# Expert weights issued by SyncE instead of ScalarE in the routing, the fourth group held until the first rows are in

## The chip, the cores and the metric

The kernel runs on one core of a Trainium2 chip. The time is the device time of one execution in microseconds (us). Engines: PE is TensorE, DVE is VectorE, ACT is ScalarE, POOL is GpSimd and SP is SyncE. A name with a q (ACTq, SPq) is an engine's instruction queue, where it issues transfers or waits.

## The reference

Eight layers in a row work on x, 1250 rows of 512 numbers: four graph convolutions and, behind each, a feed-forward layer. Each adds its result to x. Three of the feed-forward layers send rows to experts (a mixture of experts):

```
L0_ffn: attention; 64 experts (512 -> 256 -> 512), top 2 of a softmax, 78 places each; y weighted by the gates
L2_ffn: 8 experts (512 -> 512 -> 512), the best one only, no limit of places
L3_ffn: attention; 8 experts (512 -> 256 -> 512), top 2, 250 places each, each row keeps its last expert
```

In each of them the router's logits are xn @ wr, a softmax and the largest entries give every row its experts, and the expert computes func(rows @ w1 + b1) @ w2 + b2.

## The kernel before

The program is a sequence of blocks. In a block every engine has an instruction stream of its own, and the streams wait for each other by semaphores; at a block's end all engines meet. A routed layer has three blocks that matter here.

`norm_rows` norms the rows and transposes them. In L0_ffn and L3_ffn its ACT stream also issues the load that brings x back from a copy in DRAM (L404).

`route` (L1098) computes the assignment. SP writes the normed rows to DRAM (L1173, 2.5 MB in two transfers) and waits for them (L1174). PE makes the logits (L1181), DVE takes the maxima off (L1231), ACT makes the exponentials (L1216), DVE continues from L1233 with sums, the largest entries, one-hot masks (L1253) and the residual (L1916), PE counts places (L1191, L1192), DVE and PE make the list of rows of each unit (L1295, L1202), and ACT copies the gates (L1219). ACT's stream begins with `early(act)` (L1214), which is `issue_first` of the weights.

`experts` (L1434) works in units. A unit is two sets of R rows (R is 78 in L0_ffn, 125 in L2_ffn and L3_ffn). POOL gathers each set from the DRAM copy with one indirect transfer into `xb` (L1532); in L0_ffn and L3_ffn four units are gathered ahead, in L2_ffn one. PE transposes the rows (L1612), DVE moves them to `xbT` (L1684, in L2_ffn L1680), PE multiplies by w1 (L1623), ACT applies the function (L1657), PE multiplies by w2 (L1632), DVE copies out (L1693) and POOL scatters the result (L1542). In L0_ffn and L3_ffn PE transposes the second unit ahead of the products of the first (`run_ahead`, L1485); in L2_ffn, where the number of units is only known at run time, there is one unit at a time.

Weights lie in a ring of four groups (`ExpertBuffers`, L1394). A group is two experts in L0_ffn (four transfers of 512 KB), one expert in L2_ffn (two of 1 MB) and in L3_ffn (two of 512 KB). A group serves one unit in L0_ffn and L3_ffn, and one or more in L2_ffn. `issue_first` (L1423) issues the table b1 and three groups: 13 transfers in L0_ffn, 7 in L2_ffn and in L3_ffn. The fourth group, and later each group that has been used up, is issued by ACT in its loop in `experts` (`weights`, L1646), the fourth as the first thing of the block, since its semaphore `w_used` is raised there at once (L1599, L1600).

Of the kernel before, what the change touches and what calls it, by code (L numbers as in the profile page):

```python
# [352 lines left out]
def in_two(dst, src):  # L353

    return [(dst[0:120], src[0:120]), (dst[120:P], src[120:P])]
# [318 lines left out]
def attention(nc, k, x1, w_qk, b_qk, Vall, ctxT, room, spare, spare_free, late_loads, sums_dram):  # L674
# [11 lines left out]
    with ExitStack() as ctx:  # L686
# [62 lines left out]
        with nc.Block() as block:  # L749
# [245 lines left out]
            def _(v):  # L995
# [63 lines left out]
                def invert(h):  # L1059

                    v.wait_ge(sums_in, h * 32 + 32)
                    v.reciprocal(sums[:, 1, :], sums[:, 0, :]).then_inc(inv_ready, 1)
# [32 lines left out]
                take_projections(1, 1)  # L1095
                schedule(v, tiles, between)
                invert(*last[0])
def route(nc, k, yT, wr, br, E_, topk, cap, keep_last, r, rows_in, early=None, meanwhile=None):  # L1098

# [3 lines left out]
    with ExitStack() as ctx:  # L1105
# [47 lines left out]
        with nc.Block() as block:  # L1153
            @block.gpsimd
            def _(pool):
                pool.iota(ioE[:, :], [[1, E_]], base=0, channel_multiplier=0,
                          allow_small_or_imprecise_dtypes=True).then_inc(iotas, 1)

                for c in range(topk):
                    pool.iota(token1[:, c, :], [[P, T]], base=c * N + 1, channel_multiplier=1,  # L1160
                              allow_small_or_imprecise_dtypes=True).then_inc(iotas, 1)
                pool.iota(ioR[:, :], [[1, R]], base=0, channel_multiplier=0,
                          allow_small_or_imprecise_dtypes=True).then_inc(iotas, 1)
                pool.iota(no_row[:, :], [[R, NB]], base=r.unused + 1, channel_multiplier=1,
                          allow_small_or_imprecise_dtypes=True).then_inc(iotas, 1)
                if cap is None:
                    pool.iota(ioU[:, :], [[R, NB]], base=0, channel_multiplier=0,
                              allow_small_or_imprecise_dtypes=True).then_inc(iotas, 1)

            @block.sync  # L1170
            def _(sp):
                for to, what in in_two(rowtiles(r.rows_dram), rows_in):
                    sp.dma_start(to, what).then_inc(r.rows_out, 16)  # L1173
                sp.wait_ge(r.rows_out, 32)  # L1174

            @block.tensor
# [33 lines left out]

            @block.scalar
            def _(act):
                if early is not None:
                    early(act)  # L1214
                act.wait_ge(shifted, 1)
                act.activation(W[:, :, :], L[:, :, :], ACT.Exp).then_inc(exps, 1)  # L1216
                act.wait_ge(gT_done, 1)
                for n, (c0, cn) in enumerate(CH):
                    act.activation(r.gateT[:, c0:c0 + cn], ps[0:E_, 5 + n, 0:cn], ACT.Copy).then_inc(gT_out, 1)  # L1219
# [174 lines left out]
class ExpertBuffers:  # L1394
# [16 lines left out]
        self.b1s = sb("b1s", [128, E_, self.FC])  # L1411
        self.w_in = [ctx.enter_context(k.semaphore(nc, k.name(f"w_in{g}"))) for g in range(self.RING)]

    def issue(self, act, i, g):

        for x_ in range(self.EPG):
            e, slot = (i * self.RING + g) * self.EPG + x_, g * self.EPG + x_
            act.dma_start(self.w1s[:, slot, :, :], self.w1[bass.ds(e, 1)].rearrange("o p c f -> p (o c) f"))\
                .then_inc(self.w_in[g], 16)
            act.dma_start(self.w2s[:, slot, :, :], self.w2[bass.ds(e, 1)].rearrange("o (c p) n -> p (o c) n", p=128))\  # L1420
                .then_inc(self.w_in[g], 16)

    def issue_first(self, act):  # L1423

        act.dma_start(self.b1s[:, :, :], self.b1).then_inc(self.w_in[0], 16)
        for g in range(self.RING - 1):
            self.issue(act, 0, g)

    def loaded(self, eng, i, g):

# [3 lines left out]
def experts(nc, k, r, wts, func, affine, y_dram, dynamic, x, b2, Y, out=None):  # L1434
# [13 lines left out]
    with ExitStack() as ctx:  # L1448
# [15 lines left out]
        rows_loaded = [[k.gpsimd_dma_semaphore(nc, "rows") for _ in range(2)] for _ in range(DEEP)]  # L1464
# [9 lines left out]
        def group(eng, i, g, body):  # L1474

            e = i * RING + g
            if dynamic:
                n = eng.snap(eng.value_load(r.tab[0:1, 0, bass.ds(e, 1)], min_val=1, max_val=N // (2 * P)))
                first = eng.snap(eng.value_load(r.tab[0:1, 1, bass.ds(e, 1)], min_val=0, max_val=r.max_blocks))
                with eng.Fori(0, n) as q:  # L1480
                    body(i, first + q, g)
            else:
                body(i, e, g)
# [31 lines left out]
        def second(s):  # L1515
            return s if EPG == 2 else 0

        with nc.Block() as block:
# [62 lines left out]
            def loads(eng, c):  # L1581
                eng.wait_ge(all_stored, 1)
                src = rowtiles(y_dram[c * N:c * N + N, :])
                for h in range(PIECES):
                    for to, what in in_two(Y[c][:, TP * h:TP * h + TP, :], src[:, TP * h:TP * h + TP, :]):
                        eng.dma_start(to, what).then_inc(got[h], 16)  # L1586
# [57 lines left out]
            @block.scalar  # L1644
            def _(act):
                def weights(i, g):  # L1646
                    act.wait_ge(w_used[g], i + 1)
                    wts.issue(act, i, g)

                def hidden_at(i, g):  # L1650

                    def hidden(i, u, g):
                        for s in range(2):
                            act.wait_ge(h_done[s], u + 1)
                            e = (i * RING + g) * EPG + second(s)
                            for m in range(FC):
                                act.activation(hT[:, s, m, :], ps[:, 4 * s + 1, R * m:R * m + R], func,  # L1657
                                               bias=wts.b1s[:, bass.ds(e, 1), m]).then_inc(h_out[s], 1)
                    group(act, i, g, hidden)

                with act.Fori(0, ROUNDS - 1) as i:
                    for g in range(RING):
                        weights(i + (1 if g else 0), (g + RING - 1) % RING)
                        hidden_at(i, g)
                weights(ROUNDS - 1, RING - 1)
                for g in range(RING):
                    hidden_at(ROUNDS - 1, g)
                if K_ == 2:
                    loads(act, 1)
# [76 lines left out]
def rowtiles(ap):  # L1746

    return ap.rearrange("(t p) n -> p t n", p=P)
# [119 lines left out]
def transformer(nc, k, a, x128, pre, E_, F, cap, func, keep_last, rows_dram, y_dram, x_spill, sums_dram, out=None):  # L1868

    with ExitStack() as ctx:  # L1870
# [39 lines left out]
        with ExitStack() as c4:  # L1910
            wts = ExpertBuffers(nc, k, c4, E_, F, R, 1 if R == cap else 2, a[pre + "w1_p"], a[pre + "b1_p"],
                                a[pre + "w2"], Room(Gf))

            def add_residual(v):
                v.wait_ge(x_back, 32)
                v.tensor_tensor(x[:, :, :], x[:, :, :], res[:, :, :], ALU.add)  # L1916
            route(nc, k, xnT, wr, br[:, :] if bias else None, E_, 2, cap, keep_last, r, yn, wts.issue_first, add_residual)
            experts(nc, k, r, wts, func, (g2, b2), y_dram, False, x, b2r[:, :], (res, yn), out)
# [273 lines left out]
def l2_ffn(nc, k, a, x, rows_dram, y_dram):  # L2192

    E_, F = 8, 512
    with ExitStack() as ctx:
        def sb(c_, name, shape):
            return c_.enter_context(nc.sbuf_tensor(k.name(name), shape, fp32))
        xn, xT = sb(ctx, "xn", [P, T, D]), sb(ctx, "xT", [128, C, N])
        b2r, wr, br = sb(ctx, "b2r", [E_, D]), sb(ctx, "wr", [128, C, E_]), sb(ctx, "br", [1, E_])
        norm_rows(nc, k, x, xn, xT, have_stats=True, beside=[(wr[:, :, :], kchunks(a["L2_ffn_Wr"])), (br[:, :], row(a["L2_ffn_br"])),  # L2200
                                            (b2r[:, :], a["L2_ffn_b2"])])
        r = Routing(nc, k, ctx, E_, 1, None, P, rows_dram)
        with ExitStack() as c4:
            wts = ExpertBuffers(nc, k, c4, E_, F, P, 2, a["L2_ffn_w1_p"], a["L2_ffn_b1_p"], a["L2_ffn_W2"])
            route(nc, k, xT, wr, br[:, :], E_, 1, None, False, r, xn, wts.issue_first)
            experts(nc, k, r, wts, ACT.Relu, None, y_dram, True, x, b2r[:, :], (xn,))
# [338 lines left out]
```

## Time and profile before

| | us |
|---|---|
| median of 3 runs | 3326.5 (3324.61 to 3326.77) |
| profiled execution | 3323.3 |
| its span in the trace | 3321.5 |
| PE busy (share of the span) | 2699.4 (81%) |
| DVE busy | 1683.2 (51%) |
| ACT busy | 943.7 (28%) |
| POOL busy | 277.6 (8%) |
| mean granted TensorE clock | 0.891 |

Busy times are sums over all stages, and each stage has its own limit. Instructions that issue transfers are not counted as busy. The routing of L0_ffn starts at about 1267.6 in the span, that of L2_ffn at 2206.7 and that of L3_ffn at 3137.8. In a row, a bracket gives the idle time of the engine ahead of the group and what ended it.

### The profile page before, as it was taken

What the parts mean: (1) busy time and instruction counts of PE and PEld (TensorE: products, weight loads), DVE (VectorE), ACT (ScalarE), POOL (GpSimd) and SP (SyncE); (2) the same over time, 40 slices, a digit from 0 to 9 for tenths busy, and PEclk for the clock granted to TensorE, in tenths of its full rate; (3) what the DMA queues carried; (4) which work ended last, traced back from release to release, by engine and by line L of the source; (5) the groups of instructions that cost most, each with busy time, mean ns of one, the idle gap of its engine ahead of it and who ended that gap; (6) DMA issues with size and microseconds to landing.
All of it is one profiled execution on the core that took longest, in us unless ns stands there. A gap on an engine that the chain in (4) does not pass through costs nothing. (4 is left out here: it accounts for less than half of the span.)

```text
span 3321.5 us, 41255 instructions
## 1 busy us (share of the span) xinstructions
PE 2699.4 (81%) x12659; PEld 1899.7 (57%) x12660; DVE 1683.2 (51%) x3356; ACT 943.7 (28%) x2087; POOL 277.6 (8%) x273
## 2 busy tenths in 40 slices
PE   5888869985899984999688599967877579999775
PEld 3555555554778853666365266665644457877452
DVE  6777752133788834444533722241132458886344
ACT  1222230102577731111111022210111237777100
POOL 0000000000000001444000000002210000000031
PEclk9999979997899986999798799967978789999767
DMA  3000041202000005798413130033333110000334
GB/s 103 1 0 0 0 141 39 60 4 65 13 23 18 16 9 181 262 303 296 113 46 128 27 74 13 0 108 101 99 83 60 44 34 19 18 19 13 99 117 117
DMA packets 113512, 237.85 MB, mean 72 GB/s; under 512 B 32500, under 2 KB 33860, under 8 KB 112130
## 3 DMA queue, kind: packets, MB, share of 16 engines
q10 hardware_dynamic: 47350, 126.49, 12.8%
q1 hardware_dynamic: 41740, 82.14, 8.5%
q0 software_dynamic: 24320, 27.90, 2.9%
q8 instruction: 60, 0.98, 0.1%
q14 instruction: 42, 0.34, 0.0%
HBM read 189.78 MB, written 52.58 MB: 73 GB/s over the span
## 5 line engine op out<-in xcount | busy, mean ns | idle before, releaser
L1050 DVE TENSOR_REDUCE mx<-ps 125x1 f32<-125x500 f32 (+1 forms) x480 | 274.0, 588 | 57.0 <-PE ps L820 40.2
L243 PE MATMUL ps<-onehot_src,onehot_dst 125*128 x1200 | 257.7, 353 | 42.1 <-DVE onehot_dst L219 16.9
L945 ACT ACTIVATE probs_hi<-ps 125x500 fp32r<-125x500 f32 (+1 forms) x480 | 255.4, 532 | 123.8 <-DVE probs_lo L1002 79.1
L218 DVE TENSOR_SCALAR onehot_src<-iota,src_f 125x1250 f16 x400 | 217.4, 544 | 108.6 <-PE ps L243 95.7
L947 ACT ACTIVATE x<-ps 125x500 f32<-125x500 f32 (+1 forms) x480 | 258.7, 539 | 0.0
L1002 DVE TENSOR_TENSOR probs_lo<-x,probs_hi 125x1250 fp32r<-125x1250 f32 x160 | 240.2, 1501 | 35.8 <-ACT x L947 32.2
L1693 DVE COPY yb<-ps 78x512 f32<-78x512 f32 (+1 forms) x100 | 68.9, 689 | 325.7 <-PE ps L1632 325.7
L243 PEld LDWEIGHTS ps<-onehot_src,onehot_dst 125*128 x1200 | 120.9, 102 | 172.5 <-issue 117.7
L1632 PE MATMUL ps<-w2s,hT 128*78 128x512 f32 (+1 forms) x480 | 215.9, 596 | 1.9 <-ACT hT L1657 1.9
L820 PE MATMUL ps<-K_hi_lo,Q_hi_twice 128*125 128x500 f32 (+1 forms) x480 | 181.3, 384 | 23.0 <-DVE mx L1050 17.8
L828 PE MATMUL ps<-Q_hi_twice,K_hi_lo 128*125 128x500 f32 (+1 forms) x480 | 178.9, 373 | 17.9 <-ACT Q_lo_max L935 5.1
L1657 ACT ACTIVATE hT<-ps,b1s 128x78 f32<-128x78 f32 (+1 forms) x240 | 67.0, 342 | 408.3 <-PE ps L1623 408.2
L978 POOL TENSOR_TENSOR room<-room 64x600 f32 (+1 forms) x16 | 32.6, 2040 | 1780.3 <-DMA inv<-sums 1780.3
L829 PE MATMUL ps<-Q_lo_max,K_hi_one 65*125 65x500 f32 (+1 forms) x480 | 176.1, 368 | 0.0
L836 PE MATMUL ps<-probs_hi,V_hi 125*128 125x500 f32 (+1 forms) x480 | 174.0, 362 | 0.0
L837 PE MATMUL ps<-probs_hi,V_lo 125*128 125x500 f32 (+1 forms) x480 | 165.5, 360 | 0.0
L1773 PE MATMUL ps<-w,xT 128*125 128x512 f32 x320 | 145.8, 618 | 16.8 <-ACT xT L2121 8.9
L424 PE MATMUL ps<-ident,xn 125*128 125x125 f32 x280 | 45.9, 344 | 139.5 <-DVE xn L394 139.5
L1623 PE MATMUL ps<-xbT,room 128*128 128x78 f32 (+1 forms) x1280 | 154.6, 281 | 0.6 <-issue 0.6
L1623 PEld LDWEIGHTS ps<-xbT,room 128*128 128x128 f32 x1280 | 151.2, 197 | 2.3 <-issue 2.3
L219 DVE SCALAR_TENSOR_TENSOR onehot_dst<-iota,dst_f,w_parts x400 | 137.1, 343 | 0.0
L1632 PEld LDWEIGHTS ps<-w2s,hT 128*78 128x78 f32 (+1 forms) x480 | 76.5, 168 | 103.0 <-issue 101.1
(368 smaller groups left out, 4783.4 us busy)
## 6 DMA issues: line engine op xcount, KB each, us to landing
room<-in_L_ffn_w_p ACTq DMA_DIRECT2D x72, 512.0 KB, 6.0
w2s<-in_L_ffn_w ACTq DMA_DIRECT2D x72, 512.0 KB, 8.4
G<-c_spill ACTq DMA_DIRECT2D x2, 5859.4 KB
tv<-in_L_ffn_tv_W_p SPq DMA_DIRECT2D x2, 4096.0 KB
w1s<-in_L_ffn_w_p ACTq DMA_DIRECT2D x8, 1024.0 KB, 4.9
w2s<-in_L_ffn_W ACTq DMA_DIRECT2D x8, 1024.0 KB, 9.5
w_spill<-W SPq DMA_DIRECT2D x5, 1171.9 KB
c_spill<-CT ACTq DMA_DIRECT2D x1, 5859.4 KB
```

Source lines behind the costliest of these rows:

```text
L218: v.tensor_scalar(ohs[:, slot, :].rearrange("p o n -> p (o n)"), io16[:, 0:N], sF[:, bass.ds(tile, 1)], None, ALU.is_equal)
L243: mm_ = pe.matmul(ps[:, 3 * half + c, 0:cn], ohd[:, slot, :].rearrange("p o n -> p (o n)"), ohs[:, slot, c0:c0 + cn].rearrange("p o n -> p ...
L820: pe.matmul(ps[0:P, SQ + cc % 2, 0:cn], Q1[:, j, P * t:P * t + P], K1[:, j, c0:c0 + cn], start=True, stop=True).then_inc(s_done, 1)
L828: pe.matmul(o, K1[:, j, P * t:P * t + P], Q1[:, j, c0:c0 + cn], start=True, stop=False)
L829: pe.matmul(o, K2[:, j, P * t:P * t + P], Q2[:, j, c0:c0 + cn], start=False, stop=True)\
L836: pe.matmul(ps[:, ACC + n, 0:cn], VH[:, t, :], PH[:, t % 2, c0:c0 + cn], start=(t == 0), stop=False)
L945: act.activation(PH[:, t % 2, c0:c0 + cn], ps[0:P, ST + n, 0:cn], ACT.Exp, scale=SCALE).then_inc(p_hi, 1)
L947: act.activation(PT[:, t % 2, c0:c0 + cn], ps[0:P, ST + n, 0:cn], ACT.Exp, scale=SCALE).then_inc(p_out, 1)
L1002: v.tensor_tensor(PL[:, t % 2, :], PT[:, t % 2, :], PH[:, t % 2, :].bitcast(fp32), ALU.subtract)\
L1050: v.tensor_reduce(mx[:, t, n:n + 1], ps[0:P, SQ + cc % 2, 0:cn], AX.X, ALU.max)\
L1623: mm = pe.matmul(ps[:, 4 * s + 1, R * m:R * m + R], wts.w1s[:, w, c, 128 * m:128 * m + 128], xbT[:, s, parity, c, :], start=(c == 0), stop ...
L1632: mm = pe.matmul(ps[0:R, 4 * s + 2, :], hT[:, s, m, :], wts.w2s[:, w, m, :], start=(m == 0), stop=(m == FC - 1))
```

## The change

`early` is called in SP's stream, behind the issues of the row store and ahead of the wait for it, and no longer at the head of ACT's stream. In `experts` ACT waits, ahead of its loop, for both sets of rows of the first unit; its first issue behind that wait is the fourth group of weights. All three routed layers are changed.

```diff
-def route(nc, k, yT, wr, br, E_, topk, cap, keep_last, r, rows_in, early=None, meanwhile=None):
+def route(nc, k, yT, wr, br, E_, topk, cap, keep_last, r, rows_in, early, meanwhile=None):
...
                 for to, what in in_two(rowtiles(r.rows_dram), rows_in):
                     sp.dma_start(to, what).then_inc(r.rows_out, 16)
+                early(sp)
                 sp.wait_ge(r.rows_out, 32)
...
             @block.scalar
             def _(act):
-                if early is not None:
-                    early(act)
                 act.wait_ge(shifted, 1)
...
-    def issue_first(self, act):
-
-        act.dma_start(self.b1s[:, :, :], self.b1).then_inc(self.w_in[0], 16)
+    def issue_first(self, sp):
+
+        sp.dma_start(self.b1s[:, :, :], self.b1).then_inc(self.w_in[0], 16)
         for g in range(self.RING - 1):
-            self.issue(act, 0, g)
+            self.issue(sp, 0, g)
...
+                for s in range(2):
+                    act.wait_ge(rows_loaded[0][s], 16)
                 with act.Fori(0, ROUNDS - 1) as i:
                     for g in range(RING):
                         weights(i + (1 if g else 0), (g + RING - 1) % RING)
```

`issue` has the name of its first argument changed from `act` to `eng` and is otherwise as it was.

## Rows read from the trace of the kernel before

**Rows 1.** Order of time, routing of L0_ffn: start us, duration us, engine, line, tiles, count.

```profile
1267.61 2.21 SPq L1173 DMA_DIRECT2D rows<-yn  x2
...
1278.46 0.82 DVE L1231 TENSOR_TENSOR logits<-pos,m 125x640 f32<-125x640 f32 x1
...
1284.81 1.28 ACT L1216 ACT_TABLE_LOAD   x1 [17.46 <-issue]
1286.10 0.74 ACT L1216 ACTIVATE work<-logits 125x640 f32<-125x640 f32 x1
1286.87 0.82 DVE L1233 TENSOR_REDUCE m<-work 125x10 f32<-125x640 f32 x1 [7.58 <-ACT work L1216]
```

**Rows 2.** Order of time, start of the experts of L0_ffn, and PE's fourth unit.

```profile
1316.35 0.35 ACTq L1418 DMA_DIRECT2D room<-in_L_ffn_w_p  x1
1316.57 1.16 POOL L1532 DMA_INDIRECT xb<-rows,take  x1 [48.24 <-issue]
...
1320.55 0.96 POOL L1532 DMA_INDIRECT xb<-rows,take  x1 [0.30 <-issue]
...
1329.31 7.04 PE L1623 MATMUL ps<-xbT,room 128*128 128x78 f32 x32
...
1358.18 3.74 PE L1623 MATMUL ps<-xbT,room 128*128 128x78 f32 x32
```

**Rows 3.** Order of time, routing of L2_ffn and start of its experts.

```profile
2219.28 1.28 ACT L1216 ACT_TABLE_LOAD   x1 [12.88 <-issue]
...
2228.33 0.24 DVE L1231 TENSOR_TENSOR logits<-pos,m 125x80 f32<-125x80 f32 x1
2228.60 0.27 ACT L1216 ACTIVATE work<-logits 125x80 f32<-125x80 f32 x1 [8.04 <-DVE logits L1231]
...
2257.33 1.24 POOL L1532 DMA_INDIRECT xb<-rows,unit  x1 [0.97 <-POOL unit L1525]
2258.88 1.22 POOL L1532 DMA_INDIRECT xb<-rows,unit  x1 [0.30 <-issue]
...
2267.39 1.93 PE L1612 MATMUL ps<-ident,xb 125*128 125x125 f32 x8 [13.02 <-DMA xb<-rows,unit]
```

**Rows 4.** Order of time, routing of L3_ffn and start of its experts.

```profile
3161.72 0.27 ACT L1216 ACTIVATE work<-logits 125x80 f32<-125x80 f32 x1 [11.79 <-DVE logits L1231]
...
3189.86 1.27 POOL L1532 DMA_INDIRECT xb<-rows,take  x1 [51.43 <-issue]
...
3194.48 1.21 POOL L1532 DMA_INDIRECT xb<-rows,take  x1 [0.30 <-issue]
...
3202.29 5.47 PE L1623 MATMUL ps<-xbT,room 128*128 128x125 f32 x32
```

**Rows 5.** Transfer issues, us to landing: first gather of L0_ffn, L2_ffn and L3_ffn.

```profile
xb<-rows,take POOLq DMA_INDIRECT x1, 7.2
...
xb<-rows,unit POOLq DMA_INDIRECT x1, 10.0
...
xb<-rows,take POOLq DMA_INDIRECT x1, 7.7
```

**Rows 6.** Same, median: L0_ffn from 1327.5, 1350 to 1580; L2_ffn from 2275; L3_ffn 3196 to 3205.

```profile
xb<-rows,take POOLq DMA_INDIRECT x2, 4.7
...
xb<-rows,take POOLq DMA_INDIRECT x52, 6.8
...
xb<-rows,unit POOLq DMA_INDIRECT x16, 5.3
...
xb<-rows,take POOLq DMA_INDIRECT x6, 5.7
```

**Rows 7.** Busy us by stretch; then granted clock, DMA share, GB/s.

```profile
1297.00:1316.00 19.00, 10.41 (x89) 9.87 (x88) 15.44 (x28) 1.32 (x3) 0.00 (x0) 0.62 0.00 0
1329.00:1336.00 7.00, 7.00 (x36) 7.00 (x35) 2.17 (x8) 1.82 (x3) 0.07 (x1) 0.50 0.26 60
2208.00:2214.00 6.00, 6.00 (x32) 5.87 (x32) 0.00 (x0) 0.00 (x0) 0.00 (x0) 0.60 0.98 216
```

More of the change, by code:

```diff
@@ L1412, in __init__, with issue @@
         self.w_in = [ctx.enter_context(k.semaphore(nc, k.name(f"w_in{g}"))) for g in range(self.RING)]
-    def issue(self, act, i, g):
+    def issue(self, eng, i, g):
         for x_ in range(self.EPG):
             e, slot = (i * self.RING + g) * self.EPG + x_, g * self.EPG + x_
-            act.dma_start(self.w1s[:, slot, :, :], self.w1[bass.ds(e, 1)].rearrange("o p c f -> p (o c) f"))\
+            eng.dma_start(self.w1s[:, slot, :, :], self.w1[bass.ds(e, 1)].rearrange("o p c f -> p (o c) f"))\
                 .then_inc(self.w_in[g], 16)
-            act.dma_start(self.w2s[:, slot, :, :], self.w2[bass.ds(e, 1)].rearrange("o (c p) n -> p (o c) n", p=128))\
+            eng.dma_start(self.w2s[:, slot, :, :], self.w2[bass.ds(e, 1)].rearrange("o (c p) n -> p (o c) n", p=128))\
                 .then_inc(self.w_in[g], 16)
-    def issue_first(self, act):
-        act.dma_start(self.b1s[:, :, :], self.b1).then_inc(self.w_in[0], 16)
+    def issue_first(self, sp):
+        sp.dma_start(self.b1s[:, :, :], self.b1).then_inc(self.w_in[0], 16)
         for g in range(self.RING - 1):
-            self.issue(act, 0, g)
+            self.issue(sp, 0, g)
     def loaded(self, eng, i, g):
```

## The prediction

> **What bounds the kernel now.** One core runs some thirty stages one after another. TensorE is busy for 81% of the span, but what this change can move lies where TensorE stands idle, so I read the page first for the size of the whole and then the order of time of three short stretches: the three routings (in L0_ffn, L2_ffn and L3_ffn) and the start of the experts behind each. In these, every wait that ends last was looked up.
>
> In the routing of L0_ffn the reader sees a straight chain on VectorE and one gap in it. The maxima are taken off the logits (L1231) from 1278.46 for 0.82 us, so the exponential may start at 1279.3. ScalarE is not there: it is still issuing the b1 table and three groups of weights, 13 transfers, 17.46 us of "issue"; then it loads its table (1.28 us), and only at 1286.10 runs Exp. VectorE stood idle 7.58 us [rows 1]. In the other two routings the same issuing is hidden: the products of the router take so long that ScalarE waits for VectorE, 8.04 us in L2_ffn [rows 3] and 11.79 us in L3_ffn [rows 4]. The table load there follows the issuing at once and ahead of the wait (2219.28 against 2228.60), so it hides as well [rows 3].
>
> At the start of the experts all three stand still for one thing: the gathered rows. In L0_ffn GpSimd issues at 1316.57 and the first products start only at 1329.31 [rows 2]. In L2_ffn the PE waits 13.02 us for its first rows [rows 3]. In each case ScalarE issued the fourth group of weights just ahead of the gathers (1316.35 against 1316.57), so 2 MB in L0_ffn and L2_ffn, 1 MB in L3_ffn, run beside the first rows. The first gathers take 7.2, 10.0 and 7.7 us to land [rows 5]; ones with little or nothing beside them take 4.7, 5.3 and 5.7 us [rows 6].
>
> **Part 1: the issuing moves to SP.** On ScalarE 13 + 7 + 7 issues go away. In L0_ffn Exp can start 0.03 us behind L1231, as it does in L2_ffn (2228.33 + 0.24, then 2228.60) [rows 3]: 1279.28 + 0.03 + 0.74 + 0.03 puts L1233 at 1280.08 against 1286.87 [rows 1]. That is 6.8 us. The table load moves to about 1267.7, under the router's products. VectorE's chain from there to the end of the routing has no other wait that this time could run into: the residual is added meanwhile (its x was fetched in the stage ahead of the routing), and the rest alternates between VectorE and PE. I count 6.8 us in full, and 0 for the 7 issues in each of L2_ffn and L3_ffn, whose cover is 8.04 and 11.79 us.
>
> SP pays for it. It issues the two pieces of the row store, then the 13 (7, 7) weights, and only then waits for the store. Were its issues as slow as ScalarE's, it would be through at 1267.6 + 2.21 + 17.2 = 1287, while the routing ends at about 1308.5 in the new time: 21 us of cover. Nobody else waits for SP before that end. The weights now stand behind the store on one queue. In the six microseconds from 2208, when the store of L2_ffn was most of the traffic, 216 GB/s moved; even if store and weights (2.5 + 6.3 MB) went at that rate to the end, the last group would be in 41 us behind 1267.6, at 1309, and the first products of the experts want the first group only at about 1320. Today DMA is at rest from 1297 on [rows 7]. Cost: 0 (between 0 and, if the cover went, microsecond for microsecond).
>
> **Part 2: the fourth group waits for the first unit's rows.** Times from GpSimd's first gather (t0).
>
> L0_ffn: gathers start at 0 and, the fourth, 3.98 us; so the second at about 1.4 [rows 2]. At 4.7 us each [rows 6] the first unit is there at 6.1, ScalarE issues until about 8, and the second unit's last rows, issued before that but landing beside its first packets, come at 3.98 + 5.2 = 9.2. The value 5.2 is mine: from 4.7 (quiet) to 6.8, the median of the 52 gathers beside a steady stream of weights [rows 6]. With 1.1 us of transposes the products start at t0 + 10.3 where they started at 12.74 [rows 2]: 2.4 us, between 0.8 and 2.9.
>
> L2_ffn: both gathers of the unit (0 and 1.55 us) precede the products and no other does. 1.55 + 5.3 + 1.0 for the last four transposes = 7.9, against 10.06 for the landing and 1.9 for the eight transposes, 11.9 in all [rows 3, 6]: 4.0. The first gather of a stage may start slower than later ones, so 3.8, between 2 and 4.7.
>
> L3_ffn: 1 MB only was in the way. The fourth gather starts 4.62 us behind the first, + 5.7 + 1.1 of transposes = 11.4, against 12.43 to the products [rows 4, 6]: 1.0, between 0 and 2.
>
> What stands behind the new wait on ScalarE: the fourth group's issues (1.85 us in L0_ffn, four of about 0.4 with their gaps), then the activations of the first unit. Those need the PE's first products, at t0 + 10.3 or later; ScalarE is free again at 6.1 + 1.85 = 8, so nothing is late. The fourth group itself is first read by the fourth unit, whose products started 41.6 us behind t0 (1358.18) [rows 2]; issued at 6 to 8 and landing in at most ten or so, it has over 20 us in hand. Cost: 0.
>
> The Trainium skill's page "DMA: Bandwidth & Descriptors" (Anatomy of one DMA) gives 2.0 us plus the bytes at 436 GB/s for a GpSimd transfer; an estimate by it is 2.4 to 2.6 us for such a gather. By that the three starts would give some 7 us more in all, 3305 us. No row here supports it: the quiet ones took 4.7 us and more [rows 6].
>
> **The sum.** 6.8 + 2.4 + 3.8 + 1.0 = 14.0 us. The profiled execution took 3323.3 us (span 3321.5 and 1.8 around it), so 3309.3; the median of the runs shown is 3326.5, 3.2 above it, and carrying that along the forecast is 3312.5 us, 0.42% faster.
>
> **The rivals.**
> A. *The gathers don't get quicker.* Their 7 to 10 us could be the first use of the queue in a stage rather than the weights: in each case only the first gathers are slow, and they are first as well as crowded. For it: in L3_ffn 1 MB and in L0_ffn 2 MB give nearly the same (7.7, 7.2) [rows 5]. Against: the steady gathers beside weights also take longer (6.8) than quiet ones (4.7) [rows 6]. Only the 6.8 us remain: 3319.7. Chance 0.14.
> B. *The 7.58 us gap is handed on.* VectorE arrives 6.8 us sooner, but something in the routing holds its end: SP still at its issues, or the store's landing. Then only the starts gain, 7.2 us: 3319.3. Against: 21 us of cover. Chance 0.05.
> C. *The PE's clock helps too.* The first unit of L0_ffn runs at a granted clock of 0.50, the lower level of 1.2 GHz [rows 7], and its 32 products take 7.04 us against 3.74 in the fourth unit [rows 2]. If less idle time ahead kept the higher level, the unit would gain up to the 3.3 us there, and the first unit of L3_ffn, whose 32 take 5.47 us [rows 4], somewhat less than 2: 3307. Against: even quiet, seven microseconds stay idle ahead of it. A small shift either way (1 to 2 us) is likelier and is in my range. Chance 0.08.
> D. *Slower: weights late behind the store.* On one queue the first group could reach the chip after the experts ask for it. It decides once it lands later than t0 + 10 (1320), and makes the whole slower by 0.2% only from 1341 on (14.0 + 6.7 us later); the queue would then have averaged some 120 GB/s over 73 us. Against: 216 GB/s [rows 7]. It would give about 3334. The same skill page (Queues, rings and completion order) says that each DMA engine takes a queue's descriptors in order and alternates between queues, so it speaks for the weights starting later; no run shows yet how much. Chance 0.03.
>
> **How the numbers follow.** The forecast has 0.70: 14.0 us with bounds 6.8 + 0.8 + 2 + 0 = 9.6 and 6.8 + 2.9 + 4.7 + 2 = 16.4, two more either way for the clock, 3308 to 3319. With the upper end drawn out to A and B and the lower to C: 3307 to 3320. About 0.2% (6.7 us, 3319.8) is what a measurement of this kernel can tell from no change. A sits on that edge and gives half of its chance to "same"; part of B too. Faster 0.88, same 0.09, slower 0.03.
>
> **What would show it.** Right: in the routing of L0_ffn Exp starts within 0.1 us of L1231's end and the routing is some 7 us shorter; SP carries the 13 issues and is through well before it; ScalarE issues the fourth group 6 to 7 us behind t0; the first gather lands in 5 us or so; the PE's wait in L2_ffn shrinks from 13 to about 9 us. Wrong: gathers still at 7 to 10 us with no weights under way (A); SP the last to end the routing (B); a PE wait for w_in in front of L1623 (D).

## The result, and the profile after

Six executions of each, alternating on one chip: 3305.2 us after (3298.2 to 3308.0) against 3325.6 before (3319.9 to 3329.5). The ratio is 0.9942, 95% interval 0.9932 to 0.9951: 19.3 us faster, 16.3 to 22.6. The forecast was 14.0 us and 3312.5; the time lies 1.8 us below the range. The profiled execution took 3304.6 us, with a span of 3302.6 and a mean granted clock of 0.895.

The routing of L0_ffn in the order of time, changed kernel (the edit moves most line numbers up by one: L1231 is L1230 now, L1623 is L1622):

```profile
1267.18 1.75 SPq L1173 DMA_DIRECT2D rows<-yn  x2
1267.19 1.28 ACT L1215 ACT_TABLE_LOAD   x1 [0.27 <-PEq L377]
...
1268.98 2.60 SPq L1424 DMA_DIRECT2D b1s<-in_L_ffn_b_p  x1
...
1278.04 0.83 DVE L1230 TENSOR_TENSOR logits<-pos,m 125x640 f32<-125x640 f32 x1
...
1278.90 0.74 ACT L1215 ACTIVATE work<-logits 125x640 f32<-125x640 f32 x1 [10.42 <-DVE logits L1230]
1279.67 0.82 DVE L1232 TENSOR_REDUCE m<-work 125x10 f32<-125x640 f32 x1 [0.80 <-ACT work L1215]
...
1288.04 0.59 SPq L1419 DMA_DIRECT2D w2s<-in_L_ffn_w  x1
```

The 7.58 us in front of the sum of the exponentials [rows 1] are 0.80 now, which is Exp itself. The engine that waits has changed: ScalarE stands 10.42 us for VectorE. SP's last issue is at 1288.04, twenty microseconds ahead of the end of the block.

The start of the experts of L0_ffn, same view:

```profile
1309.38 1.16 POOL L1531 DMA_INDIRECT xb<-rows,take  x1 [41.48 <-issue]
...
1312.85 0.78 PE L1611 MATMUL ps<-ident,xb 78*128 78x78 f32 x4 [6.11 <-DMA xb<-rows,take]
1313.36 0.95 POOL L1531 DMA_INDIRECT xb<-rows,take  x1 [0.30 <-issue]
...
1314.48 0.41 ACTq L1417 DMA_DIRECT2D room<-in_L_ffn_w_p  x1
...
1317.08 7.03 PE L1622 MATMUL ps<-xbT,room 128*128 128x78 f32 x32
```

The first gather starts 42.2 us behind the first issue of the row store, where it took 48.96 [rows 1, 2]. The fourth group of weights leaves 5.1 us behind it, once both sets are in. The products start 7.70 us behind it, against 12.74.

In L2_ffn both gathers come first now as well:

```profile
2246.56 1.24 POOL L1531 DMA_INDIRECT xb<-rows,unit  x1 [0.97 <-POOL unit L1524]
2248.11 1.22 POOL L1531 DMA_INDIRECT xb<-rows,unit  x1 [0.30 <-issue]
...
2251.58 1.09 PE L1611 MATMUL ps<-ident,xb 125*128 125x125 f32 x4 [7.99 <-DMA xb<-rows,unit]
...
2253.00 0.37 ACTq L1417 DMA_DIRECT2D w1s<-in_L_ffn_w_p  x1
```

PE's wait of 13.02 us [rows 3] is 7.99 and 0.30. The landing of the first gathers of L0_ffn, L2_ffn and L3_ffn (median us from issue), where it was 7.2, 10.0 and 7.7 [rows 5]:

```profile
xb<-rows,take POOLq DMA_INDIRECT x1, 3.4
...
xb<-rows,unit POOLq DMA_INDIRECT x1, 5.0
...
xb<-rows,take POOLq DMA_INDIRECT x1, 5.4
```

To see what each layer gave I cut the span at the `std` activations (L400) that norm the rows at the head of the layers. In L0_ffn they stand at 1255.70 and 1634.85 before, at 1255.27 and 1624.01 after. Three profiles of the kernel before and four of the changed one (this pair and repeats, below):

| us | before | changed |
|---|---|---|
| start of the span to L0_ffn | 1255.7, 1254.6, 1258.1 | 1255.3, 1261.2, 1256.2, 1257.1 |
| L0_ffn | 379.2, 379.0, 378.4 | 368.7, 368.8, 368.0, 368.8 |
| L2_ffn | 280.8, 280.7, 280.8 | 273.9, 273.9, 273.7, 270.5 |
| L3_ffn to the end | 195.8, 195.8, 197.6 | 194.2, 194.5, 195.8, 192.5 |

What lies between L0_ffn and L2_ffn, and between L2_ffn and L3_ffn, differs by less than 1 us. The means give 10.3 us in L0_ffn, 7.8 in L2_ffn (6.9 in three of the four) and 2.1 in L3_ffn. The first row has no edit in it, and still it varies by over 6 us between executions: much of the scatter of a single time is from there, and none of the gain.

### The profile page after: what moved, and what is told of

Read it like the earlier page. It is cut to its first block and busy times, and to the rows that moved or that the text cites. A ratio compares the mean times of both kernels' runs of the same rounds, so it can differ in the third digit from the quotient of the medians.

```text
span 3302.6 us, 41258 instructions
## 1 busy us (share of the span) xinstructions
PE 2694.3 (82%) x12659; PEld 1893.4 (57%) x12660; DVE 1684.6 (51%) x3356; ACT 943.7 (29%) x2087; POOL 278.1 (8%) x273
## 3 DMA queue, kind: packets, MB, share of 16 engines
q10 hardware_dynamic: 41158, 110.67, 11.8%
## 5 line engine op out<-in xcount | busy, mean ns | idle before, releaser
L1050 DVE TENSOR_REDUCE mx<-ps 125x1 f32<-125x500 f32 (+1 forms) x480 | 273.9, 589 | 56.6 <-PE ps L820 40.4
L1622 PE MATMUL ps<-xbT,room 128*128 128x78 f32 (+1 forms) x1280 | 154.2, 280 | 0.6 <-issue 0.6
L1622 PEld LDWEIGHTS ps<-xbT,room 128*128 128x128 f32 x1280 | 150.8, 197 | 2.3 <-issue 2.3
```

What stands on the lines that cost most here:

```text
L1050: v.tensor_reduce(mx[:, t, n:n + 1], ps[0:P, SQ + cc % 2, 0:cn], AX.X, ALU.max)\
L1622: mm = pe.matmul(ps[:, 4 * s + 1, R * m:R * m + R], wts.w1s[:, w, c, 128 * m:128 * m + 128], xbT[:, s, parity, c, :], start=(c == 0), stop ...
```

## The experiments

**One part alone.** `e_move` is the changed kernel without the wait: SP issues in the routing, the fourth group leaves at once. `e_wait` is the kernel before with the wait alone.

```diff
 e_move, against the changed kernel
-                for s in range(2):
-                    act.wait_ge(rows_loaded[0][s], 16)
 e_wait, against the kernel before
+                for s in range(2):
+                    act.wait_ge(rows_loaded[0][s], 16)
                 with act.Fori(0, ROUNDS - 1) as i:
```

> Only the issuing moves to SyncE; ScalarE issues the fourth group at once, without the new wait. Theory 1 (the gain is 6.8 us from the issuing in the routing of L0_ffn and some 10 us from the three starts of the experts, which come from the new wait alone; what is left over is TensorE's clock, which falls differently in each execution): 6.8 us faster than before, ratio 0.998; the exponential starts within 0.1 us of L1230's end, the first products of L0_ffn start 12.5 us behind the first gather as they did before. Theory 2 (moving the weights behind the row store has a gain of its own, which the forecast left out): 9 to 12 us faster, with something beside the exponential shorter in all three routings.

> Only the wait in front of the fourth group; ScalarE still issues the first three in the routing. Theory 1: the products start about 5.0 us (L0_ffn), 4.6 us (L2_ffn) and 0.4 us (L3_ffn) sooner behind the first gather, 10 us in all, ratio 0.997; the exponential of L0_ffn is as late as before. Theory 2: 7 us or less, since part of what was seen at the starts came with the other queue.

`e_move` took 3318.2 us, ratio 0.9984 (0.9975 to 0.9993): 5.3 us faster, 2.3 to 8.3. `e_wait` took 3309.9, ratio 0.9960 (0.9946 to 0.9973): 13.3 us faster. Together 18.6, close to the 19.3 of both. For `e_move` the 6.8 of Theory 1 lies in the interval and the 9 to 12 of Theory 2 doesn't. `e_wait` was expected at 10 us, inside the interval of 9.0 to 18.0. In its profile L2_ffn gained 5 us beyond its start (last row; see the repeats) and the logits of L3_ffn 2.5, while L0_ffn kept 3.1 us of the 5.4 that its milestones gained. The stretches say which milestone each moves:

| us | before | e_move | e_wait | changed |
|---|---|---|---|---|
| L0_ffn, row store to first gather | 48.96 | 42.19 | 48.31 | 42.20 |
| L0_ffn, first gather to first products | 12.74 | 12.38 | 8.02 | 7.70 |
| L2_ffn, first gather to first products | 11.93 | 11.87 | 7.40 | 7.28 |
| L2_ffn, whole | 280.8 | 281.0 | 270.9 | 273.9 |

In the first three rows each part does its own thing and, to 0.7 us, none of the other's. Order of time of `e_move`, then of `e_wait`, at the start of L0_ffn's experts:

```profile
1308.91 0.41 ACTq L1417 DMA_DIRECT2D room<-in_L_ffn_w_p  x1
1309.13 1.16 POOL L1531 DMA_INDIRECT xb<-rows,take  x1 [41.47 <-issue]
...
1315.76 0.78 PE L1611 MATMUL ps<-ident,xb 78*128 78x78 f32 x4 [9.27 <-DMA xb<-rows,take]
...
1321.51 5.76 PE L1622 MATMUL ps<-xbT,room 128*128 128x78 f32 x26
```

```profile
1318.09 1.16 POOL L1532 DMA_INDIRECT xb<-rows,take  x1 [47.60 <-issue]
...
1321.57 0.78 PE L1612 MATMUL ps<-ident,xb 78*128 78x78 f32 x4 [6.11 <-DMA xb<-rows,take]
...
1326.11 6.19 PE L1623 MATMUL ps<-xbT,room 128*128 128x78 f32 x28
```

With the weights issued just ahead of it, the first rows reach PE 6.6 us behind the gather; without them, 3.5. The gather is the first one of its stage in both, so rival A (slow because first) is out.

**Who has to issue.** `e_after_exp` leaves the issuing with ACT and puts it behind Exp; the fourth group leaves at once.

```diff
 e_after_exp, against the kernel before
-                if early is not None:
-                    early(act)
                 act.wait_ge(shifted, 1)
                 act.activation(W[:, :, :], L[:, :, :], ACT.Exp).then_inc(exps, 1)
+                if early is not None:
+                    early(act)
```

> The kernel before, with ScalarE issuing its three groups right behind the exponential instead of ahead of it; no SyncE issues, no new wait. Theory 1 (the gain in the routing is only that ScalarE is free when the logits come): the exponential of L0_ffn starts 11.7 us behind the row store and the first gather 42.2 us, as with the move to SyncE; 6.8 us faster than before, ratio 0.998, and starts of the experts as before (12.4, 11.9, 12.5 us). Theory 2 (the queue behind the store has a part in it): less than 5 us, or a later first gather, since the weights go out 12 to 22 us later here.

3314.7 us, ratio 0.9972 (0.9963 to 0.9982), so 9.3 us faster (6.0 to 12.3). Order of time; the row store is at 1268.00:

```profile
1279.72 0.74 ACT L1214 ACTIVATE work<-logits 125x640 f32<-125x640 f32 x1 [10.42 <-DVE logits L1231]
1279.72 0.40 ACTq L1425 DMA_DIRECT2D b1s<-in_L_ffn_b_p  x1
...
1310.19 1.16 POOL L1532 DMA_INDIRECT xb<-rows,take  x1 [41.47 <-issue]
```

The first gather is 42.19 us behind the store, the same as with SP, and L0_ffn takes 370.8 us (`e_move` 371.7). What counts for the routing is that Exp isn't behind the issues; who issues doesn't. The 4 us between the times of the two kernels, measured on two chips with intervals that overlap, I don't read.

**The dose.** `e_half`: ACT issues half of the fourth group at once and the other half behind the wait. Its first round is written out ahead of the loop, which itself saves time in L0_ffn (below).

```diff
 e_half, against the changed kernel: issue takes a part of a group, round_of as in e_all4 below, and
...
+                act.wait_ge(w_used[RING - 1], 1)
+                wts.issue(act, 0, RING - 1, (0, EPG))
                 for s in range(2):
                     act.wait_ge(rows_loaded[0][s], 16)
...
+                wts.issue(act, 0, RING - 1, (EPG, 4))
+                round_of(0, True)
+                if ROUNDS > 2:
+                    with act.Fori(1, ROUNDS - 1) as i:
+                        round_of(i, False)
```

> The changed kernel, but half of the fourth group (one of two experts in L0_ffn, w1 alone in L2_ffn and L3_ffn) goes out at once beside the first gathers and the other half waits for the rows. Theory 1 (the first rows are slow in proportion to the weights under way): first products 10 to 10.5 us behind the first gather in L0_ffn (7.7 with none, 12.7 with 2 MB) and 9.5 us in L2_ffn (7.3 and 11.9); L3_ffn between 11.4 and 12.5; total 5 to 6 us slower than the changed kernel. Rival: a threshold, any weights ahead of the gathers cost all of it (12 us) or the first MB costs nothing (7.7 us).

3305.3 us, ratio 0.9943 (0.9929 to 0.9956). I had expected a total 5 to 6 us above the changed kernel; that was missed, since I hadn't reckoned with what the written-out round gives. The milestone answers the question: products at 9.41 us behind the first gather in L0_ffn and 9.25 in L2_ffn with 1 MB in the way, against 7.7 and 7.3 with none and 12.7 and 11.9 with 2 MB. In L2_ffn that is near half of the loss for half of the bytes, in L0_ffn a third. The 9.41 us are less than the 10 to 10.5 that I expected of L0_ffn. The delay grows with the bytes ahead; it isn't made by their mere presence.

**All four groups early.** `e_all4`: SP issues the fourth group in the routing too; no wait, and ACT's first round is written out without it. `e_again` is the changed kernel unchanged, on the same chip; `e_all4_b` repeats `e_all4` on another.

```diff
 e_all4, against the changed kernel
-        for g in range(self.RING - 1):
+        for g in range(self.RING):
             self.issue(sp, 0, g)
...
-                for s in range(2):
-                    act.wait_ge(rows_loaded[0][s], 16)
-                with act.Fori(0, ROUNDS - 1) as i:
+                def round_of(i, first):
                     for g in range(RING):
-                        weights(i + (1 if g else 0), (g + RING - 1) % RING)
+                        if g or not first:
+                            weights(i + (1 if g else 0), (g + RING - 1) % RING)
                         hidden_at(i, g)
+                round_of(0, True)
+                if ROUNDS > 2:
+                    with act.Fori(1, ROUNDS - 1) as i:
+                        round_of(i, False)
```

> SyncE issues all four groups in the routing and ScalarE neither waits nor issues ahead of the first unit (its first round is written out without the fourth group). Theory 1: gathers meet no weights at all, neither in the first nor in the second unit: first gathers land in 3.4 us (L0_ffn), 5.0 (L2_ffn) and 5.4 (L3_ffn) as with the wait; the total is within 1 us of the changed kernel, 17 to 18 us faster than before. Rival A of the prediction (first gathers are slow because they are first): it was refuted by the changed kernel unless the wait itself matters; then they would be slow here, 7 to 10 us, and the total only 7 us faster than before.

> The changed kernel once more, for what differs between two executions of one program. Theory 1: the routing of L0_ffn from the row store to the first gather and the three starts repeat within 0.3 us of those in the first trace (42.2 us; 7.7, 7.3 and 12.0 us from first gather to first products), while stretches without any edit, such as the logits of L3_ffn (2.4 us shorter than before) and the units of L2_ffn, come out 1 to 3 us different. Theory 2 (these are effects of the change): they repeat too. Ratio to before 0.994 by either.

> All four groups in the routing once more, beside the others on one chip: within 1 us of the changed kernel by Theory 1, 17 us faster than before; some 4 us better than the changed kernel if its first median was more than luck.

`e_all4` 3303.0 us (3298.7 to 3304.2), `e_again` 3308.3 (3307.2 to 3310.7): ratios 0.9938 (0.9924 to 0.9952) and 0.9953 (0.9940 to 0.9967), and no execution of the one reaches those of the other. In the profile of `e_again` the first gather (42.18 us) and the starts (8.15, 7.40 and 11.74 us) repeat to 0.5 us, where I had said 0.3. But L2_ffn (273.9) and the logits of L3_ffn (21.2) repeat too, which I had expected of the rival theory alone (see the repeats). `e_all4_b` took 3301.1, ratio 0.9927 (0.9913 to 0.9940). The starts are those of the changed kernel (7.73 and 7.81 us in L0_ffn, 7.30 and 7.33 in L2_ffn; in L3_ffn 11.30 and 11.32, where the changed kernel has 11.7 to 12.5), so the first unit's gathers are quiet either way; yet L0_ffn takes 364.7 and 364.8 us in place of 368.7. `e_peel` asks where these 4 us come from: it keeps the wait and the late fourth group and only writes out the first round.

```diff
 e_peel, against the changed kernel: round_of as in e_all4, and
                 for s in range(2):
                     act.wait_ge(rows_loaded[0][s], 16)
+                weights(0, RING - 1)
+                round_of(0, True)
```

> The changed kernel with ScalarE's first round of the experts written out and the rest as it was, the wait and the late fourth group included. In the kernel with all four groups in the routing L0_ffn is 4 us shorter than in the changed one, and it has 2 table loads in L1656 where the changed one has 8. If it is the table load at the head of each loop round (0.46 us per round): 365.3 us from norm to norm here against 368.6, table loads 2. If it is the early fourth group: 368.6 us here.

3301.9 us in one execution, L0_ffn 365.0, though its products start 9.09 us behind the first gather: the fourth gather, issued 0.7 us ahead of the weights, took 4.42 us. The view by line of ACT's activations in the experts, for the changed kernel, then `e_all4`, then `e_peel`:

```profile
L1656 ACT ACT_TABLE_LOAD  x8: 1283/1283/1283, 1320.8 to 3178.2; - x8
```

```profile
L1656 ACT ACT_TABLE_LOAD  x2: 1283/1283/1283, 1305.8 to 3165.5; - x2
```

```profile
L1656 ACT ACT_TABLE_LOAD  x2: 1283/1283/1283, 1318.6 to 3177.0; - x2
```

As long as the loop holds the first activation of the block, its body reloads the table in every round; with a round written out ahead, it doesn't. Every fourth unit of L0_ffn is 0.46 us shorter then (8.96 to 8.50, from one unit's first product by w2 to the next one's). So the gain of `e_all4` is the loop's table load and not the earlier group.

**Idle time ahead of the first products.** `e_warm` is `e_all4` with 14 products of the unit matrix, written to a bank that nothing reads, while PE waits for the first rows.

```diff
 e_warm, against e_all4
+                for _ in range(14):
+                    pe.matmul(ps[:, 3, 0:128], k.ident[:, :], k.ident[:, :], start=True, stop=True, skip_group_check=True)
                 run_ahead(pe, turn, products, after=lambda g: pe.drain().then_inc(w_used[g], 1))
```

> All four groups in the routing, and 14 extra 128x128 transposes of the identity into an unused bank at the head of the experts' TensorE stream, which no result reads, while the rows are under way. Rival C of the prediction in pure form: if the granted clock stays at its higher level, the first unit of L0_ffn (12.9 us from first products to the next unit) takes 8 to 9 us, that of L2_ffn at most 0.5 us less and L3_ffn about 1 us less, 4 to 6 us in all. Other theory: the clock is at its lower level whatever stands there, and the extra work changes nothing; if it runs longer than the wait for the rows it costs up to 2 us.

3297.8 us (3292.8 to 3302.8), ratio 0.9920 (0.9906 to 0.9933); its interval overlaps that of `e_all4_b`, on the same chip, so the 3 us aren't shown to be a gain. In L0_ffn the extra products don't hold the clock: stretches of `e_warm`, with the granted clock behind the five engines' busy time:

```profile
1309.00:1311.00 2.00, 2.00 (x12) 2.00 (x11) 0.00 (x0) 0.00 (x0) 1.70 (x2) 0.51 0.40 125
1317.00:1325.00 8.00, 8.00 (x29) 6.13 (x29) 0.31 (x2) 1.08 (x4) 2.30 (x3) 0.50 0.25 78
```

The granted clock is at 1.00 from 1313 to 1315, while PE transposes rows with gaps between, and at 0.50 again under the products. In L2_ffn they do: the first unit's 64 products take 7.31 us in place of 8.57. But five later units are slow there where the changed kernel has three, and L2_ffn takes 274.4 us, no less than 273.9.

**Repeats.** `e_before_1` and `e_before_2` are the kernel before, `e_again_2` and `e_again_3` the changed one, all on one chip.

> The kernel before, profiled again. In ten profiles so far the logits of L3_ffn (from the row store to L1231) took either 21.2 us (the changed kernel twice, the wait alone, half of the group, the extra transposes) or 23.7 us (before, the move alone, issuing behind the exponential, all four groups twice). Theory 1 (the granted clock falls a little sooner or later, by chance): both values come up in repeats of one program. Theory 2 (a systematic effect of the edit, 2.4 us of the gain): 23.7 us here each time.

> The changed kernel, profiled a third time. Logits of L3_ffn: Theory 1 either value; Theory 2 21.2 us. The starts of the experts and the routing of L0_ffn repeat to 0.5 us by both.

> The kernel before, profiled a third time. Theory 1: the logits of L3_ffn take 21.2 or 23.7 us by chance. Theory 2: 23.7 us.

> The changed kernel, profiled a fourth time. Theory 1: the logits of L3_ffn take 21.2 or 23.7 us by chance. Theory 2: 21.2 us.

They took 3322.2, 3306.8, 3327.5 and 3301.4 us; their stretches stand in the table above. The first gather of L0_ffn and the starts of the three experts' blocks lie within 0.5 us of those in the first profiles; the start of L0_ffn is 12.6 to 13.0 us before and 7.7 to 8.2 after. L2_ffn as a whole comes out at 280.7 or 280.8 in every profile of the kernel before, and at 273.7 to 273.9 or 270.5 in the changed one: steps, not scatter. Order of time, products by w1 in L2_ffn, kernel before:

```profile
2269.26 8.07 PE L1623 MATMUL ps<-xbT,w1s 128*128 128x125 f32 x64
2287.56 9.04 PE L1623 MATMUL ps<-xbT,w1s 128*128 128x125 f32 x64 [0.34 <-DVE xbT L1680]
2304.83 7.41 PE L1623 MATMUL ps<-xbT,w1s 128*128 128x125 f32 x64 [0.51 <-DVE xbT L1680]
2322.46 8.73 PE L1623 MATMUL ps<-xbT,w1s 128*128 128x125 f32 x64 [0.22 <-DVE xbT L1680]
...
2359.68 8.89 PE L1623 MATMUL ps<-xbT,w1s 128*128 128x125 f32 x64 [0.34 <-DVE xbT L1680]
```

and the changed kernel:

```profile
2253.84 8.57 PE L1622 MATMUL ps<-xbT,w1s 128*128 128x125 f32 x64
2272.65 7.41 PE L1622 MATMUL ps<-xbT,w1s 128*128 128x125 f32 x64 [0.34 <-DVE xbT L1681]
...
2306.04 7.41 PE L1622 MATMUL ps<-xbT,w1s 128*128 128x125 f32 x64 [0.30 <-DVE xbT L1681]
2323.84 7.41 PE L1622 MATMUL ps<-xbT,w1s 128*128 128x125 f32 x64 [0.34 <-DVE xbT L1681]
2341.92 8.96 PE L1622 MATMUL ps<-xbT,w1s 128*128 128x125 f32 x64 [0.34 <-DVE xbT L1681]
```

The same 64 products take 7.4 us in some units and 8.6 to 9.0 in others. Behind the first unit five of nine are long in all three profiles of the kernel before, three in three of the changed one, and one in `e_again_3` and in `e_wait`. At 1.6 us each, two fewer are 3.2 us.

**Does the start place them?** `e_delay4` and `e_delay9` are the changed kernel with 4 or 9 writes of zeros by GpSimd into an unused tile (`idle`, whose declaration is left out here) ahead of the first gather of L2_ffn alone.

```diff
 e_delay4 (e_delay9: range(9)), against the changed kernel
+                if dynamic:
+                    for j in range(4):
+                        pool.memset(idle[:, 512 * j:512 * j + 512], 0.0)
```

> The changed kernel; in L2_ffn alone GpSimd fills an unused tile with four memsets ahead of its first gather, a delay of its start of some 2 us. Theory 1 (the extra 2.8 us of L2_ffn come from where the clock's dips fall among its ten units, and that follows the time at which the first products start): the number of units whose w1 products take 8.6 to 9.0 us instead of 7.4 changes from 3 towards 5, and the stage (norm to norm) takes more than the delay added to 273.9 us, or less. Theory 3 (they come from the queues: no weights beside the gathers also later): still 3 such units, 273.9 us plus the delay exactly.

> The same with nine memsets, a delay of some 4.5 us, which puts the first products of L2_ffn about where the kernel before has them. Theory 1: five stretched units and 280.8 us, as in all profiles of before. Theory 3: 3 stretched units and 278.4 us.

They took 3322.6 and 3317.4 us in one execution each; the first has some 9 us more in L0_ffn, which its edit doesn't touch (last section). The first gather of L2_ffn came 1.8 and 4.2 us later. Delay alone would make L2_ffn 275.7 and 278.1 us; it took 277.7 and 280.7, with four and five long units behind the first. Order of time of `e_delay9`, the rows that answer to those of the kernel before above:

```profile
2263.71 8.20 PE L1626 MATMUL ps<-xbT,w1s 128*128 128x125 f32 x64
2282.20 9.04 PE L1626 MATMUL ps<-xbT,w1s 128*128 128x125 f32 x64 [0.34 <-DVE xbT L1685]
...
2317.14 8.85 PE L1626 MATMUL ps<-xbT,w1s 128*128 128x125 f32 x64 [0.25 <-DVE xbT L1685]
```

With the start back near where it was, the pattern and the 280.7 us of the kernel before are back, with the gathers as quick as ever (products 7.30 us behind the first). So the extra 2 to 3 us of L2_ffn belong to the time at which its products start, not to the gathers or the weights. (The delay also lengthens PE's wait ahead of them; the two aren't told apart.) The other profiles agree. From the `std` activation at the head of L2_ffn to the first products, and long units behind the first:

| products start, us | long units | profiles |
|---|---|---|
| 67.6 to 67.8 | 3 | changed kernel (three), `e_all4`, `e_all4_b`, `e_peel` |
| 67.6 and 67.8 | 1 | `e_again_3`, `e_wait` |
| 69.5 and 69.7 | 4 | `e_delay4`, `e_half` |
| 71.9 to 72.5 | 5 | kernel before (three), `e_move`, `e_after_exp`, `e_delay9` |

The start isn't all of it: at nearly the same start there are three or one, and `e_warm`, with 67.2 and extra products ahead, has five. What decides between them stays open.

## Why the prediction was right in direction and short in size

**Part 1 held to a tenth of a microsecond.** Exp starts 0.03 us behind the end of the maxima's subtraction, and the first gather is 6.76 us nearer to the store, against 6.8 forecast. SP was through at 1288.6 (I had 1287). The gap was not handed on (rival B). The weights did come later behind the store: the transfers came to rest between 1299 and 1301 in place of 1297 [rows 7], but the first products never waited for weights, so rival D had nothing to bite on. In L2_ffn the issuing was worth nothing, as forecast.

**Part 2 had the right mechanism and gathers that were too slow.** I took 4.7 and 5.2 us for L0_ffn from rows that I called quiet [rows 6], though the DMA share is still 0.59 from 1327.5 to 1333; with nothing beside them these gathers of 78 rows land in 3.0 to 3.5 in the changed kernel. With the fourth at 3.98 + 3.0 and its transposes the products start at 7.7, not 10.3: 5.0 us gained where I had 2.4, outside its bounds of 0.8 to 2.9 (4.8 in the mean of all profiles of the two kernels). In L2_ffn 4.7 to 5.0 us in place of 5.3 give 4.6 for 3.8. In L3_ffn the four gathers ahead of the first products took 5.2 to 6.4 us in place of 5.7, and the start gained 0.4 on that profile where I had 1.0. Net 2.8 us more than forecast. An estimate by the fit on the Trainium skill's page "DMA: Bandwidth & Descriptors" (Anatomy of one DMA) was 2.4 to 2.6 us for such a gather. This case's trace does not bear that out: 3.0 us at the least, and 4.7 and more for 125 rows. In L0_ffn it was still nearer than the rows that I chose, since I took for quiet what had the tail of other transfers beside it. In the terms of my own sum the estimate is worth 8.6 us more and not 7 (2.8, 2.7 and 3.1), so 3304. That this is near the measured 3305.2 is luck: it has gathers that are too quick and nothing from the clock.

**The clock was the other step that failed.** I set it to 0 with 2 us either way. In L0_ffn it took something back. The products by w1 of the first unit take 7.03 us as before, but those by w2 take longer. Order of time, kernel before, then changed:

```profile
1336.14 4.94 PE L1632 MATMUL ps<-w2s,hT 128*78 128x512 f32 x8
```

```profile
1323.90 5.66 PE L1631 MATMUL ps<-w2s,hT 128*78 128x512 f32 x8
```

The granted clock over the twelve microseconds from the first products is 0.54 where it was 0.59. That is 0.7 us. The rest of what turns the 11.8 us of milestones into 10.3 isn't shown to be the clock's: in the means 0.5 us of it lies behind the landing of the last scatter, where VectorE waits for rows that come back from DRAM (33.4 us to the next `std` before, 33.9 after, single profiles 32.7 to 34.2). In L2_ffn it gave: 4.6 us of start became 6.9, in one profile of four 10.3, by two (four) long units fewer; the delay experiment shows that this hangs on when the products start (or on how long PE waits ahead of them). In L3_ffn the logits end 23.7 us behind the store in all profiles of the kernel before and 21.2 to 21.3 in three of the four of the changed one. In those the clock is up for the first 3 us, which saves 2.4 us. Stretches at the head of that routing, before, then changed:

```profile
3138.00:3141.00 3.00, 3.00 (x15) 2.96 (x15) 0.00 (x0) 0.00 (x0) 0.43 (x4) 0.50 1.03 239
```

```profile
3121.00:3124.00 3.00, 3.00 (x24) 2.92 (x24) 0.00 (x0) 0.68 (x1) 0.05 (x1) 0.91 1.00 204
```

`e_again_2`, the same program, had 23.7. Whether the change makes the good case more frequent stays open: three profiles of four against none of three is too few. Over all kernels it is 7 of the 9 profiles with the new wait, and 1 of the 8 without it (`e_warm`), which points at the wait; no run shows how it would act on this stretch. Net of the three layers (less 1.5, plus 2.3, plus 1.7, with L2_ffn as in three profiles of the four) what isn't the gathers' gave some 2.5 us, of which the clock by the rows above some 3.3 (less 0.7, plus 2.3, plus 1.7) and the rest of L0_ffn less 0.8.

**Rival C** had the sign and not the mechanism: shorter idle time did not keep the level up in the first unit of L0_ffn, which got slower, and the gain came in later units of L2_ffn and in the logits of L3_ffn. In the first unit of L3_ffn it was 0.2 us (5.41 to 5.22 in the means).

**The sum.** 2.8 us from the gathers and the net 2.5, mostly the clock's, are the 5.3 between 14.0 and 19.3. The lower end of my range had 16.4 us for the edit's own work and 2 for the clock, and the gathers of L0_ffn alone passed their bound by 2.1. The rest of the distance to 3305.2 is the level of the kernel before in this comparison, 3325.6 in place of 3326.5, and the scatter of the changed one: `e_again`, on another chip, has 3308.3.

**The best version seen** (`e_warm` aside, whose further 3 us aren't shown) is the changed kernel with all four groups issued in the routing and ACT's first round written out (`e_all4`: 5.4 us below the changed kernel on the same chip). By `e_peel` the written-out round does it in L0_ffn; in L3_ffn the transposes for the next unit follow the first products by 8.0 us in `e_all4` and `e_all4_b`, and by 8.8 to 9.4 in all the others.

## What to carry to other kernels

Look for activations that stand behind a row of transfer issues in their engine's stream, and for large transfers issued just ahead of small ones that something waits for: the first costs the issuing time wherever the producer is quicker than the issues, the second up to 5 us here for 2 MB. Both can be priced apart, and here they add up. Take the duration of an undisturbed small transfer only from rows with no other traffic in the stretch. A shift of a few microseconds ahead of a long run of short PE bursts can move their clock as well, so compare whole stages over repeated profiles before putting the difference down to the edit's own mechanism.

## What the runs showed of the hardware

- *Slow bursts follow the time of the start.* In L2_ffn 64 equal products take 7.41 or 9.04 us by unit, and the pattern changes with a start put back by 4.2 us (and with extra products ahead of it). The Trainium skill's page "TensorE: Matmul & The Clock Gate" (What's actually happening) says that the number of slow matmuls differs between runs of one kernel; the trace agrees for the head of L3_ffn's routing (21.2 or 23.7 us in one program).
- *A table load of 1.28 us came back at each round of a hardware loop* whose body held the block's first activation: 8 loads against 2; without them, L0_ffn is 3.6 to 3.9 us shorter (`e_peel`, `e_all4`).
- *The cover that the change took away can be missed.* In some executions the router's products of L0_ffn run at or near the lower level of 1.2 GHz (granted clock 0.59 and 0.51 over them in the two below, 1.00 in the profile before). In `e_before_1` they took 14.54 us in place of 8.9, but ScalarE was still issuing, and Exp came no later. In `e_delay4`, whose edit is in L2_ffn only, they took 16.05, and nothing hides that in the changed kernel: its L0_ffn took 377.5 us. Order of time, `e_before_1`, then `e_delay4`:

```profile
1266.60 14.54 PE L1181 MATMUL ps<-wr,xnT 128*125 128x64 f32 x80 [2.42 <-PEq L377]
...
1283.38 1.28 ACT L1216 ACT_TABLE_LOAD   x1 [17.08 <-issue]
```

```profile
1271.33 16.05 PE L1182 MATMUL ps<-wr,xnT 128*125 128x64 f32 x80 [2.99 <-PEq L377]
...
1290.13 0.74 ACT L1215 ACTIVATE work<-logits 125x640 f32<-125x640 f32 x1 [17.55 <-DVE logits L1230]
```
